# A mixture-of-experts stage with an eight-deep ring of weight chunks, rows gathered three tiles ahead, and another order on VectorE and GpSimd

## What is computed

```python
x = x + L0_ffn(L0_cond(x))      # grouped convolution, then an NF4 feed-forward layer (hidden 2752) with LoRA
z = L1_cond(x)                  # per batch a mixed 64x64 kernel: out = agg_w @ x + agg_b
# L1_ffn, 8 experts, top 1:
selected = argmax(softmax(zf @ gate_w.T + gate_b), -1)
for j in range(8):
    out = out + where(selected == j, zf @ expert_w[j].T + expert_b[j], 0)
x = x + out
```

## Time and profile before

| | |
|---|---|
| three runs, median (lowest to highest) | 1533.24 us (1530.97 to 1535.55) |
| the profiled execution, its own time | 1532.94 us |
| its span in the trace | 1531.5 us |
| TensorE busy | 1431.8 us, 93% of the span |
| VectorE busy | 1125.8 us, 74% |
| ScalarE busy | 762.1 us, 50% |
| GpSimd busy | 155.1 us, 10% |

### The profile page before, as it was taken

How to read it: one execution, slowest core, us unless ns; L and a number is a source line. 1 busy time by engine, 2 the same in 40 slices (tenths; PEclk the granted TensorE clock), 3 DMA queues, 4 the chain that set the end, 5 groups by cost and what they waited for, 6 DMA issues and landing times.

```text
span 1531.5 us, 20837 instructions
## 1 busy us (share of the span) xinstructions
PE 1431.8 (93%) x6815; PEld 1163.4 (76%) x6815; DVE 1125.8 (74%) x1075; ACT 762.1 (50%) x845; POOL 155.1 (10%) x215
## 2 busy tenths in 40 slices
PE   6886899999999999999999999999999499999896
PEld 5576788888888888888888888888865377777674
DVE  3672787877888788787887878875244588888885
ACT  3561554464455455445445445542112266776663
POOL 0112200000000000000000000000011233343440
PEclk8898999999999999999999999999999599999998
DMA  5567565755665665575565566466555845968860
GB/s 163 201 203 277 220 219 219 264 216 194 261 232 193 233 248 199 217 270 189 215 255 223 204 235 254 186 232 212 225 197 211 272 132 138 338 167 248 307 183 2
DMA packets 104365, 331.29 MB, mean 216 GB/s; under 512 B 17361, under 2 KB 24921, under 8 KB 104249
## 3 DMA queue, kind: packets, MB, share of 16 engines
q1 hardware_dynamic: 80478, 258.22, 45.2%
q0 software_dynamic: 22512, 71.32, 15.3%
q10 hardware_dynamic: 1298, 0.68, 0.2%
HBM read 295.04 MB, written 46.14 MB: 223 GB/s over the span
## 4 chain that ended last, share of the span: by engine, by line
PE 82%; DVE 5%; DMA 4%; ACT 3%; issue 3%; ACTq 1%; POOL 1%; DVEq 0%; SPq 0%; POOLq 0%
PE pair L1072 24%; PE pair L1074 23%; PE pair L1073 23%; PE pair L1121 3%; DVE wlr L1046 2%; PE pair L1216 2%; DMA am<-am_dn 1%; PE pair L1281 1%; DMA batch_kernels<-aggs 1%; PE pair L1131 1%; DVE wf L775 1%; ACT whr L707 1%; PE pair L1223 1%; DMA zg<-z_rows,zidx 1%; PE pair L1134 1%
## 5 line engine op out<-in xcount | busy, mean ns | idle before, releaser
L775 DVE TENSOR_TENSOR wf<-wf,term 128x1024 f32<-128x1024 f32 x308 | 377.2, 1225 | 93.4 <-ACT term L568 74.5
L568 ACT ACTIVATE term<-codes 128x1024 f32<-128x1024 int32 x308 | 321.0, 1055 | 107.0 <-DVE wf L775 107.0
L1072 PE MATMUL pair<-wh,hh 128*128 128x512 f32 x704 | 275.2, 391 | 4.0 <-DVE acc L814 2.6
L1074 PE MATMUL pair<-wh,hl 128*128 128x512 f32 x704 | 274.7, 390 | 0.0
L1073 PE MATMUL pair<-wl,hh 128*128 128x512 f32 x704 | 274.6, 390 | 0.0
L1072 PE MATMUL pair<-ring,wh 128*128 128x512 f32 x656 | 255.5, 390 | 1.5 <-issue 1.5
L814 DVE TENSOR_TENSOR acc<-acc,pair 128x1024 f32<-128x1024 f32 x176 | 214.2, 1217 | 57.9 <-PE pair L1074 57.7
L1074 PE MATMUL pair<-ring,wl 128*128 128x512 f32 x656 | 255.2, 389 | 0.0
L1073 PE MATMUL pair<-ring,wh 128*128 128x512 f32 x656 | 255.2, 389 | 0.0
L596 ACT ACTIVATE wh<-wf 128x1024 fp32r<-128x1024 f32 x44 | 46.7, 1060 | 338.7 <-DVE wf L790 338.7
L1046 DVE TENSOR_TENSOR wlr<-wraw,whr 128x1024 fp32r<-128x1024 f32 x184 | 213.1, 1219 | 2.8 <-ACT whr L707 2.8
(11 more groups left out here) (165 smaller groups left out, 1386.8 us busy)
## 6 DMA issues: line engine op xcount, KB each, us to landing
ring<-x_parts SPq DMA_DIRECT2D x320, 512.0 KB, 7.7
wraw<-exp_w SPq DMA_DIRECT2D x64, 512.0 KB, 13.1
x_parts<-stage POOLq DMA_DIRECT2D x24, 512.0 KB, 8.5
xg<-exp_b POOLq DMA_DIRECT2D x23, 512.0 KB, 6.9
codes<-codes_up SPq DMA_DIRECT2D x22, 512.0 KB, 7.6
codes<-codes_dn SPq DMA_DIRECT2D x22, 512.0 KB, 6.2
am<-am_dn SPq DMA_DIRECT2D x22, 512.0 KB
acc<-x_nat POOLq DMA_DIRECT2D x16, 512.0 KB, 10.7
```

What stands on the lines that cost most here:

```text
L568: return nc.scalar.activation(out, codes[:, n % 2], ACT.Relu, scale=scale, bias=-scale * bend)
L775: nc.vector.tensor_tensor(whole(n), whole(n), term[:, e % 2], op).then_inc(term_added, 1)
L1072: mm(ps, ah, bh, start=first, stop=False)
L1074: return mm(ps, al, bh, start=False, stop=last)
```

## The change

The ring of chunks has 8 places in place of 4, for the high and for the low part, so a place is a chunk number. `zg` has four buffers and is filled three tiles ahead. On ScalarE and VectorE the rows of tile s are split behind chunk 2 of the same tile s (before: behind chunk 5 of tile s-1). VectorE's `add_rows` of the tile before stands behind chunk 7 (before: behind chunk 1). TensorE transposes the next tile's rows behind chunk 1 (before: 3). GpSimd's order in a tile is gather_z, gather_x, add_bias, scatter, and the bias is added one tile ahead.

```diff
-        whr = sb(moe, "whr", [P, 4, L], F32R)
-        wlr = sb(moe, "wlr", [P, 4, L], F32R)
+        whr = sb(moe, "whr", [P, KT, L], F32R)
+        wlr = sb(moe, "wlr", [P, KT, L], F32R)
...
             def gather_z(i, s):
-                wait(pool, tr_mm, i * 4 + s - 1)
+                wait(pool, tr_mm, i * 4 + s - 3)
...
             def tile(i, s):
                 left = NS if not isinstance(i, int) else NS - 4 * i - s
+                if left > 3:
+                    gather_z(i, s + 3)
                 if left > 2:
-                    gather_z(i, s + 2)
-                    add_bias(i, s + 2)
+                    gather_x(i, s + 2)
+                if left > 1:
+                    add_bias(i, s + 1)
                 scatter(i, s)
-                if left > 3:
-                    gather_x(i, s + 3)
-
-            gather_z(0, 0)
-            gather_z(0, 1)
+
             for s in range(3):
-                gather_x(0, s)
+                gather_z(0, s)
+            gather_x(0, 0)
+            gather_x(0, 1)
             add_bias(0, 0)
-            add_bias(0, 1)
...
             def convert_high(i, s):
-                    wait(act, chunk_mm, i * 32 + KT * s + kt - 3)
-                    nc.scalar.activation(whr[:, kt % 4], wraw[:, bass.ds(buf, 1), kt].rearrange("p a n -> p (a n)"),
+
+                    wait(act, chunk_mm, i * 32 + KT * (s - 1) + kt + 1)
+                    nc.scalar.activation(whr[:, kt], wraw[:, bass.ds(buf, 1), kt].rearrange("p a n -> p (a n)"),
                                          ACT.Copy).then_inc(whr_ready, 1)
-                    if kt == 5 and not (isinstance(i, int) and 4 * i + s == NS - 1):
-                        z_high(i, s + 1)
+                    if kt == 2:
+                        z_high(i, s)
...
             def convert_low(i, s):
-                    if kt == 1 and not (isinstance(i, int) and i == s == 0):
-                        add_rows(*before_it(i, s))
-                    if kt == 5 and not (isinstance(i, int) and 4 * i + s == NS - 1):
-                        z_low(i, s + 1)
+                    if kt == 2:
+                        z_low(i, s)
+                if not (isinstance(i, int) and i == s == 0):
+                    add_rows(*before_it(i, s))
...
             def product(i, s):
-                    if kt == 3 and not (isinstance(i, int) and 4 * i + s == NS - 1):
+                    if kt == 1 and not (isinstance(i, int) and 4 * i + s == NS - 1):
                         rows_transposed(i, s + 1)
```

More of the change, by code:

```diff
@@ L232, in program @@
         through = sb(moe, "through", [P, E], I32)
-        zidx = sb(moe, "zidx", [P, 2], I32)
+        zidx = sb(moe, "zidx", [P, 4], I32)
         xidx = sb(moe, "xidx", [P, 4], I32)
+        xg = sb(moe, "xg", [P, 4, L])
+        zg = sb(moe, "zg", [P, 4, L])
         moe.close()
@@ L269, in program @@
         zidx_ready, xidx_ready = sem("zidx_ready"), sem("xidx_ready")
-        zg_in = [sem(f"zg_in{i}") for i in range(2)]
+        zg_in = [sem(f"zg_in{i}") for i in range(4)]
         xg_in = [sem(f"xg_in{i}") for i in range(4)]
@@ L479, in gather_z @@
             def gather_z(i, s):
-                wait(pool, tr_mm, i * 4 + s - 1)
+                wait(pool, tr_mm, i * 4 + s - 3)
                 pool.sem_inc(pool_passed, 1)
-                rows = zidx[:, s % 2:s % 2 + 1]
-                if isinstance(i, int) and 4 * i + s < 2:
+                rows = zidx[:, s % 4:s % 4 + 1]
+                if isinstance(i, int) and 4 * i + s < 3:
                     rows = table[:, s:s + 1]
@@ L490, in gather_z @@
                     pool.sem_inc(pool_passed, 1)
-                pool.indirect_dma_start(zg[:, s % 2], None, z_dram, bass.IndirectOffsetOnAxis(rows, 0),
-                                        bounds_check=last_row, oob_is_err=False).then_inc(zg_in[s % 2], 16)
+                pool.indirect_dma_start(zg[:, s % 4], None, z_dram, bass.IndirectOffsetOnAxis(rows, 0),
+                                        bounds_check=last_row, oob_is_err=False).then_inc(zg_in[s % 4], 16)
             def gather_x(i, s):
@@ L714, in _ @@
             act.wait_ge(tiles_ready, TABLES)
-            z_high(0, 0)
             for i in rounds(act, NS // 4):
@@ L1045, in convert_low @@
                     dve.wait_ge(whr_ready, i * 32 + KT * s + kt + 1)
[L1046 to L1051 removed]
+                    nc.vector.tensor_tensor(wlr[:, kt], wraw[:, bass.ds(buf, 1), kt].rearrange("p a n -> p (a n)"),
+                                            whr[:, kt], ALU.subtract).then_inc(wlr_ready, 1)
+                    if kt == 2:
+                        z_low(i, s)
+                if not (isinstance(i, int) and i == s == 0):
+                    add_rows(*before_it(i, s))
             def before_it(i, s):
@@ L1057, in _ @@
             dve.wait_ge(tiles_ready, TABLES)
-            z_low(0, 0)
             for i in rounds(dve, NS // 4):
@@ L1277, in rows_transposed @@
             def rows_transposed(i, s):
-                pe.wait_ge(zg_in[s % 2], i * 32 + 16 * (s // 2 + 1))
+                pe.wait_ge(zg_in[s % 4], i * 16 + 16 * (s // 4 + 1))
                 wait(pe, ztl_ready, i * 4 + s - 1)
                 for kt in range(KT):
-                    ins = nc.tensor.transpose(pair[2 + s % 2][:, kt * P:(kt + 1) * P], zg[:, s % 2, kt * P:(kt + 1) * P], ident[:])
+                    ins = nc.tensor.transpose(pair[2 + s % 2][:, kt * P:(kt + 1) * P], zg[:, s % 4, kt * P:(kt + 1) * P], ident[:])
                 ins.then_inc(tr_mm, 1)
@@ L1291, in product @@
                         d = slice(h * 512, (h + 1) * 512)
-                        ins = three(bank[2 * (s % 2) + h], zth[:, s % 2, kt], ztl[:, s % 2, kt], whr[:, kt % 4, d],
-                                    wlr[:, kt % 4, d], kt == 0, kt == KT - 1)
+                        ins = three(bank[2 * (s % 2) + h], zth[:, s % 2, kt], ztl[:, s % 2, kt], whr[:, kt, d],
+                                    wlr[:, kt, d], kt == 0, kt == KT - 1)
                     ins.then_inc(chunk_mm, 1)
-                    if kt == 3 and not (isinstance(i, int) and 4 * i + s == NS - 1):
+                    if kt == 1 and not (isinstance(i, int) and 4 * i + s == NS - 1):
                         rows_transposed(i, s + 1)
```

2 lines of the change are left out of this document (removed).

## The result

The changed kernel takes 1507.85 us (median of four runs, 1503.95 to 1510.03) against 1533.97 (1530.97 to 1535.55): ratio 0.9829, interval 0.9801 to 0.9857. Measured again on another chip it was 1504.89 (five runs, 1504.11 to 1511.78) against 1532.73, ratio 0.9844 [0.9820, 0.9868]. Faster by 1.6 to 1.7%; the forecast was 1501.0, with 1496 to 1511 as range. The profiled execution took 1503.95 us, its span is 1502.5.

The account below looks back on a forecast made before the run. A loop of waits, 13.08 us a tile, bounds the experts; without it TensorE's 11.79. Start 1212.9 + 250.7 matmuls + 19.6 transposes + 1.7 clock + 0.2 = 1485.1; with end, residue and offsets 1501.0 us, range 1496 to 1511.

Parts of the forecast that it names:

- two of the rivals (1508 and 1510): Expert weights landing late, 1508, chance 0.10; VectorE becoming the bound at 12.2 us a tile, 1510, chance 0.10.
- The loop named in the prediction: Experts before the change: waits through transposes, both splits of the rows, chunk 6 and 36 matmuls, 13.08 us a tile.
- TensorE's floor of 11.79 a tile: TensorE without waits: 48 matmuls 10.90 us plus transposes 0.89 a tile; the new pace, saving 1.29 a tile.
- the residue: 1.0 us kept of the 2.6 lost near a late gather of z, for stretches in which weights are loaded.
- Gather of z ... worth up to 2.6: Gathering z earlier: old gathers lost 2.6 us over 21 tile distances, so the edit is worth up to that.
- Weights late: Rival, chance 0.10: first three weight chunks landing in 19.5 us make TensorE stand 3 to 4 us twice, 1508.
- 8 us of room: Chunk 7 of the next tile on VectorE: ready 8 us before TensorE needs it.
- Hidden, 5.7 to spare: GpSimd's bias: issued by about T+11.5, landing 9.0 later at worst, added by VectorE at T+26.2; 5.7 us to spare.
- "finished rows" waits for the bias: Sign in the profile, on VectorE, that the prediction would be wrong; no size given.
- the slower rival: Chance 0.03: bias issued a tile later closes a loop through finished rows and gathers; landing of 19.5 gives 1556.
- 0.46 us of slack: VectorE's ten instructions take 11.33 us a tile, 0.46 below TensorE's 11.79, so VectorE just keeps pace.
- Clock at the start: TensorE begins the experts at half clock, 8 matmuls taking 3.55 us in place of 1.8; this stays, 1.7 us.

Follow-up runs that it names:

- old order: Changed kernel with ScalarE, VectorE and TensorE back in the order before the change, keeping ring of eight and GpSimd's new transfers: 1536.27 us, ratio 1.0028.
- few weights: Changed kernel with loads of experts 2 to 7 moving only an eighth of each chunk: 1501.16 us, ratio 0.9803.
- old GpSimd order: Changed kernel with z gathered two tiles ahead into two buffers and the bias right behind the gather, as before: 1533.99 us, ratio 1.0016.
- chunk-wise release: Changed kernel with each weight chunk loaded again once that chunk of the side's last tile is used: 1501.42 us, again 1508.18; ratios 0.9799, 0.9847.
- ring of four: Changed kernel's new order with the ring of chunks back at four places: 1600.55 us, ratio 1.0445.
- rows at 1: Changed kernel with VectorE's finished rows back behind chunk 1: 1620.45 us, ratio 1.0578.

## Why the prediction was right, and where its steps were not

**The number: inside the range, above the forecast.** The medians, 1507.85 and 1504.89, are 6.9 and 3.9 us above 1501.0. The first is nearer to two of the rivals (1508 and 1510), which the range took in, than to the forecast. So the time alone does not tell them apart; the distance of 11.79 in the profiles does. The profiled executions lost 2.7 and 3.4 us in stands, but the first was the fastest of its four and the second the median of its five. What the slower ones had on top no profile shows. The range's lower end is also 1.4 us below what its own terms give (0.6 for the pitch, 1.0 and 2.0: 1497.4).

**The loop and its floor: right.** The loop named in the prediction set the pace before, and undoing its part alone brings all of it back (old order). TensorE's floor of 11.79 a tile is 11.787 in the kernel with few weights. That the whole sum, 1501.0, is 1501.16 there is in part luck: its experts' stretch is 293.8 where the forecast implies 295.4 (1499.3 - 1203.86), 1.0 of it the residue that was not needed, and the stages ahead took 2.1 us longer than in the trace that the forecast started from. Ring and order are one change: order without ring 1600, ring without order 1536.

**"Gather of z ... worth up to 2.6".** In the sum this did no harm, since the changed kernel has the gather covered. As a reading of what the edit is worth it failed: it priced the gather by what it cost in the old rhythm. In the new one the old GpSimd order costs all of the gain, 28 us against the changed kernel. I had worked out when the new gather is wanted and issued, and had not done the same for the old one. The Trainium skill's rule (DMA: Bandwidth & Descriptors, "Anatomy of one DMA — SWDGE (gpsimd) path"), an estimate of 3.2 us for a landing, is further off still: in that run the gathers of z landed in 2.1 to 10.7 us, with a median of 5.0.

**"Weights late": the rival that came true in part.** I gave it 0.10 and 7 us; the first profiled execution of the changed kernel lost 2.7 at one place, the second nothing. The step that was off is the deadline. I checked the first three chunks against the next split, and the last one against TensorE, 8 us of room. But VectorE works in order: behind chunk 7 it still has the finished rows, three chunks and the next split. From the conversion of chunk 7 to the next product are 8.3 us (1410.83 to 1419.10), so its deadline is about 24.5 us after the load's start (three products of 11.79, less the 2.6 us into a product at which the load starts, less 8.3), and it was converted 26.9 us after it (1383.95, the load's first transfer on SyncE, to 1410.83). The 2.4 us between are what TensorE stood.

**"Hidden, 5.7 to spare" for the bias: a step that failed.** In the second profile it was late by 3.69 us on VectorE, with two terms off. I had the bias issued 7.7 us behind the finished rows (T+3.8 to T+11.5); with the two slow issues ahead it was 13.4 (1280.06 to 1293.43). And I had 9.0 for its landing, by the earlier trace rows; it took 11.78. That is 8.5 us against 5.7 to spare, and VectorE was ready for it 0.8 earlier than my schedule had it. The prediction named this as a sign that it is wrong ("finished rows" waits for the bias), and by this sign it was. All three stands of that execution come from it. It is the start of the mechanism of the slower rival, and costs TensorE about 1 us each time and not 55 in all, because that needs a landing of 17 us or more in every tile.

**VectorE: 0.46 us of slack is little.** VectorE is not the bound, as forecast, and in the first profile it shows 13 waits for ScalarE, 13.6 us, not two a tile. It takes a delay of 2.7 us without TensorE noticing (3 us by the forecast), but works it off at 0.44 us a tile, so for six tiles it has less than full cover for the next delay. The third stand of the second profile is such a case: 1.24 covered, three tiles behind the second.

**Clock at the start.** The term was 1.7 us. In the first profile the first product begins 1.8 us earlier than before and its first 12 matmuls take 5.49 us (1213.19 to 1218.68 in the chain) where 2.72 is full clock, and the transposes behind them 1.22 in place of 0.87:

```profile
1218.68 1.22 PE pair L1280 x8
```

That is 3.1 us. In the second profile and in those with few weights and chunk-wise release the same 12 matmuls cost 1.6 to 1.8, as forecast. So the term holds in these four and is 1.4 short in the first. With 0.3 for the start, 1.4 for the clock and 2.7 for the late weights in place of the 1.0 of residue, the forecast of 1500.7 for the profiled execution becomes 1504.1; it was 1503.95. The clock was left out again in two expectations, for the ring of four and behind the long stands of the old GpSimd order.

## What to carry to other kernels

Find the loop before you count buffers: here the ring helped only with an order whose loop passes through it, and the order only where the ring let it run ahead. When a period shrinks, work out issue and deadline again for every transfer under the new order, the ones that the change leaves alone included, and take as deadline the first thing that stands behind the waiting instruction on its engine, not the consumer of the data. If an engine keeps 4% of slack, one delay of a few us takes many rounds to work off, and a second one that falls into them has that much less cover. Where you price a long stand of TensorE, look in the rows for what its clock did behind stands of that length.

## What the runs showed of the hardware that I had not expected

- Transfers issued by GpSimd took 3.4 us (a scatter) and 5.8 us (a gather) in place of about 1.2, one after the other: three and six times in the two profiles of the changed kernel, twice where hardly any weights were moved, once with the chunk-wise release, and never in the slower loops (ring of 4, old order, rows at 1). The cause is open.
- While GpSimd's transfers were under way, the weights came at 204 GB/s (512 KB in 2.6 us), about half of what was moved in all in the fullest microseconds of that stretch (426).
- TensorE's granted clock behind stands of about 3 us: with the ring of 4 (2.5 to 3.4 us) it was 0.57 to 0.69 over the next 4 us at 17 stands and full at five; with the rows at 1 (3.6 to 3.9 us) it was 0.50 to 0.64 at all 22. The means over these runs are 0.956 and 0.950, against 0.973.
- The stages ahead of the experts, the same code in all kernels, ended between 1125.35 and 1134.10 us (GpSimd's first instruction behind them). That spread is more than the 4.6 us that the forecast took as the bound of a measurement.
